# An attention and feed-forward kernel: the order of SP's transfers, the setup's fold of M and the fold of N in slot 1

## The reference

```python
x1 = normalise(x)
q = (layernorm(x1, ln2) @ Wq) * (1 + f) + f      # 16 heads of 64
k, v = split(layernorm(ctx, ln1) @ Wkv)
x2 = x + softmax(q @ k.T / 8) @ v @ Wout
y = x2 + tanh(normalise(x2) @ weight @ aux1 @ aux2 + bias)
```

## Time and profile before

| | |
|---|---|
| median of 3 runs | 2148.74 us (2148.23 to 2148.9) |
| the profiled execution, its own time | 2149.72 us |
| its span in the trace | 2147.9 us |
| busy PE, DVE, ACT, POOL | 96%, 70%, 62%, 64% |
| chain that ended last, PE's share | 66% |
| DMA, mean over the span | 201 GB/s |

### The profile page before, as it was taken

How to read it: one execution, slowest core, us unless ns; L and a number is a source line. 1 busy time by engine, 2 the same in 40 slices (tenths; PEclk the granted TensorE clock), 3 DMA queues, 4 the chain that set the end, 5 groups by cost and what they waited for, 6 DMA issues and landing times.

```text
span 2147.9 us, 31943 instructions
## 1 busy us (share of the span) xinstructions
PE 2061.6 (96%) x9216; PEld 1703.3 (79%) x9216; DVE 1504.6 (70%) x2387; ACT 1321.1 (62%) x2985; POOL 1377.0 (64%) x1485
## 2 busy tenths in 40 slices
PE   6986899999999999999999999999999999999997
PEld 5765777878878888887888788888888888888886
DVE  6744656666677777777676777777777777777775
ACT  3334556666676666666666666666666666666653
POOL 5433565666667676766767676776667676767563
PEclk9997999999999999999999999999999999999999
DMA  6644676777767777776767676776756566656553
GB/s 213 195 125 152 199 224 197 230 231 219 236 208 218 216 223 212 219 221 197 225 202 220 201 222 208 220 233 195 223 181 201 176 203 179 198 181 196 168 175 105
DMA packets 479503, 432.08 MB, mean 201 GB/s; under 512 B 63200, under 2 KB 353248, under 8 KB 479328
## 3 DMA queue, kind: packets, MB, share of 16 engines
q1 hardware_dynamic: 479328, 430.04, 65.7%
HBM read 251.53 MB, written 178.32 MB: 200 GB/s over the span
## 4 chain that ended last, share of the span: by engine, by line
PE 66%; SPq 8%; DMA 5%; issue 4%; DVE 4%; ACT 3%; POOL 3%; POOLq 0%; DVEq 0%; ACTq 0%
PE bank L160 28%; PE bank L1006 15%; PE bank L165 14%; PE bank L1009 8%; DMA m_scratch<-evac 3%; SPq L914 3%; SPq L933 2%; DMA wst<-wst_scratch 1%; POOL area L1169 1%; PE bank L774 1%; DVE turned L1105 1%; DVE area L1086 1%; PE bank L775 1%; DVE row_max L1091 1%; DVE bdv L631 1%
## 5 line engine op out<-in xcount | busy, mean ns | idle before, releaser
L1176 POOL TENSOR_TENSOR area<-area,row_inv 128x512 f32<-128x512 f32 x256 | 324.7, 1268 | 134.9 <-DVE row_inv L1100 134.9
L160 PE MATMUL bank<-M_hi,xT_hi 128*128 128x512 f32 x1024 | 401.3, 392 | 6.1 <-ACT xT_hi L892 6.1
L1006 PE MATMUL bank<-N_hi,pT_hi 128*128 128x512 f32 x1024 | 400.8, 391 | 0.0
L160 PE MATMUL bank<-M_lo,xT_hi 128*128 128x512 f32 x1024 | 400.4, 391 | 0.0
L1006 PE MATMUL bank<-N_lo,pT_hi 128*128 128x512 f32 x1024 | 400.1, 391 | 0.0
L1169 POOL TENSOR_TENSOR area<-area,row_max 128x256 f32<-128x256 f32 x512 | 303.5, 614 | 133.7 <-DVE row_max L1091 133.6
L1183 POOL TENSOR_TENSOR area<-area 128x512 f32<-128x512 f32 x128 | 166.2, 1299 | 339.7 <-ACT area L1045 339.7
L1037 ACT CAST pT_hi<-turned 128x512 fp32r<-128x512 f32 x256 | 159.1, 621 | 339.2 <-DVE turned L1105 339.2
L1086 DVE SCALAR_TENSOR_TENSOR area<-bank,rs,area 128x512 f32<-128x512 f32 x256 | 191.7, 749 | 171.7 <-PE bank L165 171.4
L1110 DVE TENSOR_TENSOR pT_lo<-turned,pT_hi 128x512 fp32r<-128x512 f32 x256 | 177.9, 695 | 157.3 <-ACT pT_hi L1037 157.3
L165 PE MATMUL bank<-M_hi,xT_lo 128*128 128x512 f32 x1024 | 274.9, 390 | 0.0
(11 more groups left out here) (143 smaller groups left out, 3978.3 us busy)
## 6 DMA issues: line engine op xcount, KB each, us to landing
p_scratch<-area SPq DMA_DIRECT2D x256, 256.0 KB, 2.7
p_moved<-p_scratch SPq DMA_DIRECT2D x1024, 64.0 KB, 2.2
area<-x_dram SPq DMA_DIRECT2D x128, 256.0 KB, 3.7
area<-x_turned_dram SPq DMA_DIRECT2D x128, 256.0 KB, 3.0
x_scratch<-area SPq DMA_DIRECT2D x128, 256.0 KB, 2.5
x_moved<-x_scratch SPq DMA_DIRECT2D x512, 64.0 KB, 2.4
y_dram<-area SPq DMA_DIRECT2D x128, 256.0 KB, 2.6
land<-m_scratch SPq DMA_DIRECT2D x120, 256.0 KB, 3.7
```

The lines of the kernel that those rows point to most:

```text
L160: mm = eng.matmul(ps, sh, mv, start=(n == 0), stop=False)
L1006: pe.matmul(O_ps[:], st(pT_hi, k), n_cols(mv, k), start=(k == 0 and mv is N_hi), stop=False)
L1176: pool.tensor_tensor(s, s, inv, ALU.mult).then_inc(s_p[q], 1)
```

## The change

- **Bias rows.** `bias_out` has two buffers with a semaphore each. PE's and ACT's bias work is one step later (n-19); sums 13, 14 and 15 stand at parts 0, 4 and 8 of the fold of M. `k0` is cut into two halves, at steps 26 and 28.
- **Raw buffers.** `m1_raw` is eight buffers of 128x512 (four in `stage_more`, two in `xr`, two in `S[0]`), none used twice. SP stores each once when both engines have written it: eight transfers of 256 KB for sixteen of 128 KB. After them SP issues `load_k`, `load_v(0)` and `load_xT(1)`, which were in slot 0, and then the last bias store. `load_x` of tiles 2 and 3 waits for all eight stores.
- **Slot 0.** `xT_hi` of tile 1 stands right behind exp(0), `xT_lo` of tile 1 ahead of the normalising.
- **Slot 1.** The fold of N for batch 0 moves on PE from ahead of place D to behind place A, on ACT behind exp(1), on DVE behind the sums.
- **Places.** In slots 9 to 24 the two tiles stand at C and D, not at A and C.
- **SP.** `load_wst` is taken out of `tile_store` and has its own place (`next_wst`), ahead of the store. The x2 reads stand first in the slot. The x2 write stands ahead of P's second write, and the first half of P is read ahead of store C.
- **DVE.** The transpose of x2 stands ahead of both sums.

```diff
-        k0_raw = m1_raw = stage[2]
-        ku, bias_out = ctx_in[0:2], ln2_b_row
+        k0_raw = stage[2]
+        ku, bias_out = ctx_in[0:2], (ln2_b_row, ln1_b_row)
...
+        m1_raw = [stage_more[:, i * BANK:(i + 1) * BANK] for i in range(4)] + xr[2:4] + [S[0][:, i * BANK:(i + 1) * BANK] for i in range(2)]
...
-                  24: [("k0_load", 0)], 28: [("k0", 0)], 29: [("x0", 0)]}
+                  24: [("k0_load", 0)], 26: [("k0", 0)], 28: [("k0", 1)], 29: [("x0", 0)]}
...
-            pe_steps += [("kb", n - 18)] if n >= 18 else []
+            pe_steps += [("kb", n - 19)] if n >= 19 else []
...
-            for c in range(16):
-                dc, g = m_where(c)
-                sp.wait_ge(s_m1r[c % 2], c // 2 + 1)
-                sp.dma_start(m_scratch[1, dc, g // 2, :, 2 * (g % 2) * P:2 * (g % 2) * P + 2 * P],
-                             m1_part(c)).then_inc(s_m1w[c % 4], 16)
-                if c == 4:
-                    store_bias(14)
-            store_bias(15)
+            for k in range(8):
+                dc, g = m_where(2 * k)
+                for w in s_m1r:
+                    sp.wait_ge(w, k + 1)
+                sp.dma_start(m_scratch[1, dc, g // 2], m1_raw[k]).then_inc(s_m1w, 16)
+                if k in (1, 3):
+                    store_bias(13 + k // 2)
             sp.wait_ge(s_m, 16)
             load_k(sp, 0)
+            load_v(sp, 0)
+            load_xT(sp, 1)
+            store_bias(15)
...
             act.wait_ge(s_kb, k + 1)
-            at_least(act, s_kbst, 32 * k)
-            act.copy(bias_out, kb_ps[k % 2][:]).then_inc(s_kbo, 1)
+            at_least(act, s_kbst[k % 2], 32 * (k // 2))
+            act.copy(bias_out[k % 2], kb_ps[k % 2][:]).then_inc(s_kbo, 1)
...
-                    if k >= 2:
-                        bias_evacuate(act, k - 2)
+                    if k >= 3:
+                        bias_evacuate(act, k - 3)
...
-                if c in (4, 6):
-                    bias_sums(pe, 12 + c // 2)
+                if c in (0, 4, 8):
+                    bias_sums(pe, 13 + c // 4)
...
         def m1_read(eng, c, copy):
-            if c >= 4:
-                eng.wait_ge(s_m1w[c % 4], 16 * (c // 4))
...
-            tile_at[TPB + 1 + m, "A"], tile_at[TPB + 1 + m, "C"] = 32 + 2 * m, 32 + 2 * m + 1
+            tile_at[TPB + 1 + m, "C"], tile_at[TPB + 1 + m, "D"] = 32 + 2 * m, 32 + 2 * m + 1
...
-            load_wst(sp, n + 2)
```

More of the change, by code:

```diff
@@ L234, in build @@
         s_kv, s_kvo = sem("s_kv"), sem("s_kvo")
-        s_ku, s_kuh, s_kul, s_kb, s_kbo, s_kbst = (sem(n) for n in ("s_ku", "s_kuh", "s_kul", "s_kb", "s_kbo", "s_kbst"))
+        s_ku, s_kuh, s_kul, s_kb, s_kbo = (sem(n) for n in ("s_ku", "s_kuh", "s_kul", "s_kb", "s_kbo"))
+        s_kbst = [sem(f"s_kbst{i}") for i in range(2)]
         s_kvst = [sem(f"s_kvst{i}") for i in range(2)]
@@ L299, in setup_sp @@
                                  kv_out[i % 2].rearrange("p (b j) -> p b j", b=8)).then_inc(s_kvst[i % 2], 16)
-                if step == "kv" and i >= 18:
-                    store_bias(i - 18)
+                if step == "kv" and i >= 19:
+                    store_bias(i - 19)
                 if step == "wst":
@@ L404, in setup_act @@
                     act.wait_ge(s_kz, 1)
-                    for half in range(2):
-                        last = act.copy(k0_diag(0, half), k0_dense(half))
-                    last.then_inc(s_k0h, 1)
+                    act.copy(k0_diag(0, i), k0_dense(i)).then_inc(s_k0h, 1)
         def setup_dve(dve):
@@ L490, in setup_dve @@
                 if step == "k0":
[L491 to L494, removed]
+                    dve.wait_ge(s_k0h, i + 1)
+                    dve.tensor_tensor(k0_diag(1, i), k0_dense(i), k0_diag(0, i).bitcast(F32), ALU.subtract).then_inc(s_k0l, 1)
         def bias_sums(pe, k):
@@ L577, in build @@
         s_m1r = two("s_m1r")
-        s_m1w = [sem(f"s_m1w{i}") for i in range(4)]
+        s_m1w = sem("s_m1w")
         s_k0in, s_kz, s_k0h, s_k0l, s_wstw = (sem(n) for n in ("s_k0in", "s_kz", "s_k0h", "s_k0l", "s_wstw"))
@@ L613, in load_bias @@
             at_least(sp, s_sb[1], 8 * b)
[L614 to L617, removed]
+            if b < 2:
+                for w in s_kbst:
+                    sp.wait_ge(w, 32 * (4 if b == 0 else 8))
             sp.dma_start(bias, bias_scratch[bass.ds(b, 1), :].to_broadcast([P, INNER])).then_inc(s_bin, 16)
@@ L813, in load_land @@
                     sp.wait_ge(s_vp, 1)
[L814 to L815 removed]
+                    sp.wait_ge(s_m1w, 16 * 8)
             if j % 4 == 0:
@@ L918, in write_p, with next_wst @@
                 sp.dma_start(p_scratch[t % 2][:, q * BANK:(q + 1) * BANK], half_of(S[t % 2], q)).then_inc(s_pw[q], 16)
[L920 to L925, removed]
+            def next_wst(place, u=t):
+                if (u, place) in tile_at:
+                    load_wst(sp, tile_at[u, place] + 2)
             if tile_of(t - 3):
@@ L933, in slot_sp @@
                     sp.dma_start(dst, src).then_inc(s_x2r, 16)
+            next_wst("D", t - 1)
+            if tile_of(t - 1):
+                read_p(1, t - 1)
+            if 0 < t < T - 1:
+                load_xT(sp, t + 1)
+            if t == TPB:
+                load_land(sp, t)
+            store("D", t - 1)
             if tile_of(t - 4):
@@ L939, in slot_sp @@
                 load_x(sp, t + 2, (t + 2) % RING)
-            store("D", t - 1)
+            next_wst("A")
             for kp in first_of_pair(t):
                 load_k(sp, kp + 1)
-            if m == 0 and t < T:
+            if m == 0 and 0 < t < T:
                 load_v(sp, t // TPB)
-            elif t < TPB:
+            elif 0 < t < TPB:
                 load_land(sp, t)
-            elif t + 1 < T - TPB:
+            elif TPB <= t < T - TPB - 1:
                 load_land(sp, t + 1)
@@ L953, in slot_sp @@
                 write_p(0)
-            store("B")
-            if t < T:
-                write_p(1)
+            if t != 1:
+                next_wst("B")
+                store("B")
             if tile_of(t - 2):
@@ L960, in slot_sp @@
                 sp.dma_start(x2_scratch[u % 2], xr[u % RING]).then_inc(s_x2w, 16)
+            if t < T:
+                write_p(1)
+                read_p(0, t)
+            if t == 1:
+                next_wst("B")
+                store("B")
+            next_wst("C")
             store("C")
-            if t < T:
-                read_p(0, t)
             if t == 0:
@@ L994, in slot_pe @@
             tile("A")
+            if t == 1:
+                fold_n_pe(pe, 0, range(8), lambda c: pe.wait_ge(s_sb[c], t + 1) if c < 2 else None)
             if tile_of(t - 2):
@@ L1059, in slot_act @@
                 exp(1)
+            if t == 1:
+                fold_hi(act, 0, range(8), s_n, s_nh, N_fold[2])
             evacuate("B")
-            if t + 1 < T:
+            if 0 < t < T - 1:
                 xT_split_hi(act, t + 1)
@@ L1071, in slot_act @@
                 v_prepare_act(act, t // TPB)
-            if m == 1 and t < T:
+            if m == 1 and 1 < t < T:
                 fold_hi(act, t - 1, range(8), s_n, s_nh, N_fold[2])
@@ L1138, in slot_dve @@
             if t < T:
+                inverse_sums(0)
                 inverse_sums(1)
+            if t == 1:
+                fold_lo(dve, 0, range(8), *N_fold)
             if tile_of(t - 3):
```

28 lines of the change are left out of this document (17 added, 11 removed).

## The result

The changed kernel takes 2162.84 us (median of 4 runs, 2160.63 to 2165.41), the kernel before 2148.82 on the same chip: a ratio of 1.0065, 95% interval 1.0048 to 1.0083. It is 14 us slower, where 2098 was forecast. The profiled execution took 2161.16 us, its span is 2159.4.

The account below looks back on a forecast made before the run. PE was taken as the bound, so only its waits and half-clock stretches could give time back. Terms summing to 51.0, and 1.0 for the median, came off the profiled 2149.72: 2098 us, range 2080 to 2124.

Parts of the forecast that it names:

- Setup, -18: Before the first score matmul: two bias rows and eight raw buffers remove waits for landings, 18 us less, bounds 10 and 21.
- slot 0, -2.7: Slots 0 and 1: ACT starts x's high part right behind exp(0), 2.7 us sooner.
- signs of being right: First score matmul at 164, fewer bias waits, no long `wst` waits in slots 2 to 7, evacuate D waiting about 1, full clock.
- Slots 25 on, -4: Long stage: x2 reads go ahead of five transfers, 2.4 us, cutting PE's waits for x2's high part by 4 us.
- slower rival: DVE waits for x2's reads ahead of the sums in some 117 slots: 2133 or slower than before; chance 0.06.
- "Against": Objection to DVE waiting for x2's reads: the reads leave sooner, so the wait shrinks.
- None of SP's waits ahead of a `wst` is for a landing: SP's queue: argument against the rival that setup or SP gives less (2106 each, 2114 both; chance 0.15).
- the round of slots 10 to 24: Tiles at C and D: evacuate D waits about 1 for store C, not 4.0; round 13.9, stage -9.
- Slots 3 to 8, -12: `wst` loads no longer stand behind P's reads, so PE's idle time and lost clock shrink: 12 us, bounds 4 and 15.
- Slots 1 and 2, 0 and -0.8: Slot 1's moved fold of N was given nothing (ends +2, -3); slot 2 loses its short `wst` wait, 0.8 us.
- Slot 9: Slot 9 has 2.73 us idle, its wait for x2: 2 us less.
- the end: Last W3 products: 4.9 us stays on its own chain, the wait before falls from 2.7 to 0.3; -2.5 us.

Follow-up runs that it names:

- e1: The kernel before with the setup part only (two bias rows, eight raw buffers, halves of `k0`): 2136.99 us, ratio 0.9928.
- e2: The changed kernel with the load of x at the head of SP's slot: 2136.93 us, ratio 0.9927.
- e9: e5 with x2's reads back where they stood before the change, the transpose still ahead of the sums: 2123.05 us, ratio 0.9895.
- e4: The changed kernel with the load of x at the slot's head and P's first half read behind store C: 2111.65 us, ratio 0.9812.
- e6: e4 with the two tiles of slots 9 to 24 at places A and C again: 2119.85 us, ratio 0.9857.
- e5: e4 with the fold of N at the end of slot 1 again: 2106.52 us, ratio 0.9800.
- e12: e5 with DVE's first sum ahead of the transpose and x2's write behind P's second write again: 2101.38 us, ratio 0.9796.
- e8: e4 with the write of x2 behind P's second write again: 2112.88 us, ratio 0.9828.

## Why the prediction was wrong, by its own steps

**Setup, -18, and slot 0, -2.7: right.** 17.4 and 2.7 in the trace, 15.5 for the setup alone in e1. The bias wait fell as worked out. Two of the signs of being right came, the first score matmul at 164 and these waits; the next, no `wst` wait over 1 us in slots 2 to 7, did not (longest 2.7), and slots above 14.1 came in the long stage with ACT waiting and not DVE.

**Slots 25 on, -4: the step that failed.** The prediction wrote "The x2 reads go ahead of five transfers, 2.4 us" and counted what x2 gains by it. Of the transfers that are passed it priced the reads of P's second half ("nothing") and left out the load of x, a cost put at nothing without a reason: the five, the load of x among them, go behind four reads, 1.9 us, after the four reads of P's first half had already been put ahead of store C. It looked for the price of x2's order on DVE, its slower rival, and not at the engine that consumes the passed transfer. ACT's order has x's copy directly ahead of x2's, so x late is x2 late. Measured: +26 us, 18.3 of it PE's idle time and the rest slower matmuls, two short stretches at the lower clock among them, which a sum of waits leaves out. Putting that one load in front gave 30 back (e2). The rival on DVE exists (e9: 152.3 us of waits, 18 to 20 us), but only when the reads are late, as its own "Against" said. The mechanism that decided is none of the rivals; 0.06 on slower was too little.

**"None of SP's waits ahead of a `wst` is for a landing": false.** `read_p(0, t)` waits for P's first write. Before the change store C and a `wst` stood between P's second write and the reads; put ahead of them the reads find the first write still under way. The prediction did not draw on SP's own waits; before the change they already had this line, with 9.2 us in 13 places of the long stage. Around the start of slot 12 (373.04), SP's and ACT's timelines of the changed kernel show the size:

```profile
370.70 0.43 SPq L915 DMA_DIRECT2D p_scratch<-area  x1
373.34 1.75 SPq L911 DMA_DIRECT2D p_moved<-p_scratch  x4
375.13 0.43 SPq L739 DMA_DIRECT2D wst<-wst_scratch  x1
375.61 0.43 SPq L795 DMA_DIRECT2D m_scratch<-evac  x1
```

```profile
378.34 0.59 ACT L789 COPY evac<-bank 128x512 f32<-128x512 f32 x1 [3.44 <-DMA m_scratch<-evac]
```

SP stands idle 2.2 us, from 371.13 to 373.34, until P's first write, which left at 368.62, has landed. Store C leaves 2.6 into the slot, not 0.7, and lands 2.7 later, near the 2.5 of the forecast (the median of the stage is 3.5). So the round of slots 10 to 24, worked out with "about 1" of waiting, had 3.4 here: what was missing is chiefly the wait ahead of the store. With the reads behind store C the number comes out, 237.08 to 227.05 in e4, -10.0 for the -9 forecast, but in part by luck. The prediction gave the 9 to the tiles at C and D; with the tiles at A and C and all else as in e4 (e6) the stage takes 230.5, so the places give 3.5 of the 10 and the rest of the plan 6.5. The 9.7 that the places are worth in all lie mostly in slot 25, for which the prediction had nothing of the kind.

The rule cited there (the Trainium skill, DMA: Bandwidth & Descriptors, queues, rings and completion order) would have had the store inherit what is left of the reads ahead of it. The row doesn't ask for that: 2.7 us to ACT's copy behind four reads and a `wst`; over slots 10 to 24 the stores of both places took 2.5 / 3.5 / 4.2 us, against 2.5 / 3.6 / 6.6 before. What was overlooked is in the Trainium skill too (DMA: Bandwidth & Descriptors, anatomy of one DMA, a section on transfers that GpSimd issues): the DMA engines do not wait on semaphores, and any such wait happens on the issuing sequencer before dispatch. SP's timeline above agrees for its queue: after 2.2 us idle the four reads leave, and only behind them the `wst` and store C.

**Slots 3 to 8, -12: the cover was gone.** -2.6. The `wst` of place B did leave sooner (in slot 3 5.2 us into the slot in place of 8.1), but SP waited 5.9 us in four places of this stage for P's landing; PE's wait for `wst` fell to 8.4 from 12.5. With the order repaired the stage takes 102.57 (-7.2, e4), 103.38 (-6.4, e5) and 100.19 (-9.6, e12), so the term was 2.4 to 5.6 us too large. That the `wst` loads bring what is left is argued; no run isolates them.

**Slots 1 and 2, 0 and -0.8: mis-sized.** +4.1 and +2.6. Both causes were named (ACT behind exp(1), a `wst` behind `read_p(0)`), with an end of +2, and then given nothing. Missing was that DVE, busy with the fold, turns P some 6 us late, which holds SP's reads and the `wst` behind them.

**Slot 9 (-2.7 for -2)** lies near its forecast, **the end (-0.8 for -2.5)** gave a third of it, both in a kernel whose order had moved. **The write of x2** is worth nothing (e8), as forecast.

The two overlooked waits are worth 54 us (e4). Put into the sum, they would have made 2152 of 2098, on the other side of 2148. Without them the plan comes to 2108 by its ratio on the result's chip, and without the moved fold (e5) to 2106, still 8 short of 2098.

## What to carry to other kernels

When a transfer is moved forward in a queue, price every transfer that it passes, at the engine that consumes it: how long before its use does it leave now, what does its landing take, and what else stands behind its consumer in that engine's order. A read-back from DRAM waits for the landing of the write, here 2.0 to 6.6 us, so keep between write and read as much work of the queue as there is, and put nothing urgent behind the read. Where a change bundles moves, the sign can hang on one of them: here two lines on one queue turned 0.7% slower into 1.9% faster.

## What was not expected of the hardware

Landings of one and the same kind of transfer are spread widely: P's 256 KB write took 2.0 / 2.5 / 6.6 us (shortest, median, longest) in slots 2 and on. SP's wait for it comes in 29 places only of the long stage's hundred slots; in the round of slot 78 the landing was 5.26 us, twice the median, while x's (3.12) was an ordinary one. Most slots of the long stage stayed as long as before; 25 slots grew by more than 0.15, by 28.1 together, and 23.8 of that lies in slots with m = 0 or 1, where values are loaded and N is folded. The median of x's landing hardly changed with the order (2.9 before, 3.0 after): the load was not slower, only later.
